# Last product of a four-layer graph network: high and low halves against a widened adjacency, with GpSimd's gathers in steps of two tiles

## The chip, the cores and the metric

The kernel runs on one core of a Trainium2 chip. The metric is the device time of one execution in microseconds (us); lower is better. The engines are TensorE (PE in the profile), VectorE (DVE), ScalarE (ACT), GpSimd (POOL) and SyncE (SP), which issues most of the DMAs. A difference of less than about 0.5% (9 us) can't be told from no change in a measurement of this kernel.

## The reference, cut to what matters

There are 4096 nodes with 128 features and a 4096 x 4096 adjacency `adj` of zeros and ones (about 0.4% ones, and the diagonal). Four layers follow one another, each added to `x`. The last is the one of the change:

```python
def _L3_gnn_ref(x, A, W1, b1, W2, b2, sigma, k):
    def _lap_mul(A, x):
        d = 1.0 / jnp.sqrt(jnp.sum(A, axis=-1))
        return d[:, None] * (A @ (d[:, None] * x))
    z = _lap_mul(A, x) @ W1 + b1
    z = jax.nn.leaky_relu(z, negative_slope=0.1)
    sq = jnp.sum(z * z, axis=-1)
    d2 = jnp.maximum(sq[:, None] + sq[None, :] - 2.0 * (z @ z.T), 0.0)
    S = jnp.exp(-jnp.sqrt(d2 + 1e-10) / (2.0 * sigma))
    ranks = ...
    S = jnp.where(ranks < k, S, 0.0)       # k = 4 nearest nodes of each row
    return _lap_mul(S + A, x) @ W2 + b2
```

The last line is a product with A, the same for all rows, and a sum of four rows for each node, weighted with S.

## The kernel before, in words

The nodes form 32 tiles (`NT`) of 128, and 8 groups (`NG`) of 4 tiles (`G`); t is a tile, g a group, q the tile in its group, r = g % 2. The adjacency is stored turned in DRAM (`adjT_panels`), one byte an entry, and comes back through the tile `panel`. Everything is written by hand: each engine has its own instruction list, and semaphores (`s_...`) join them. PE works through these stages: adjacency turned and first product (to about 330 us), the neighbourhood maximum (to 710), a wide product w = 0 (to 880), a panel product (to 1090), a wide product w = 1 (to 1228), the search of the four nearest (1228 to 1535), the last product (1518 to 1746).

**A panel product** (`product`, `blocks`, L707) takes one tile of 128 rows at a time: 32 matmuls, with a 128x128 block of the panel as weights and three bf16 parts of the features (3 x 128 = 384 columns) streaming. Bank q holds the result, VectorE adds its three parts (`take_product`, L1703). The parts come from ScalarE (`part0`, `part1`, L917 and L921) and GpSimd (`split`, L1323 and L1328). SyncE loads the panel of tile q of the next group when this group's tile q is done (512 KB).

**A wide product** (`wide_product`, L773) works on 512 rows (one group) at once: the features are the weights, in two halves (`layer_halves`, high and low), and the adjacency streams, 512 columns wide in fp32r. One *slot* is an eighth of it: a piece of 256 KB from DRAM, widened from one byte to four (`widen`, L1001 on ScalarE, L1520 on GpSimd) into a ring of 4 slots (`adj_ring`), then 8 matmuls, and `s_slot` tells that the slot is free. Slot n can be widened when slot n - 4 is free. After 8 slots ScalarE copies the product out (`take_wide`, L1008) and PE turns it back (`turn_back`, L784). Groups 0 and 1 are interleaved (`FIRST_PAIR`): pieces 0 to 5 of both, then (0,6), (1,6), (0,7), (1,7). A piece of group 1 goes to the place of the same piece of group 0, once that is widened.

**The last stage.** The scaled features are stored to DRAM (`last_operand`, L1233). GpSimd then gathers, for each tile, four times 128 rows of 512 bytes with indirect DMAs (`last_gathers`, L1573: 16 gathers a group, 128 in all) into `near`, which holds two groups. Before tile t's gathers it waits until VectorE has taken the products up to tile t - 3:

```python
pool.wait_ge(s_sum, NT + t + 2)
```

In `last_group`, at q = 2, GpSimd stages the indices of the next group (L1564), and for that waits until VectorE has used all gathered rows of the group before (`s_gath_used`); tile (g, q) also waits until (g - 2, q) is used. VectorE (`last`) takes the product of a tile, adds the four weighted rows (L2367 three times, L2370), and after four tiles scales, adds the bias and x, and ScalarE's queue stores the group (L1280).

Of the kernel before, what the change touches and what calls it, by code (L numbers as in the profile page):

```python
# [25 lines left out]
P = 128  # L26
# [17 lines left out]
ON_POOL = ((1, 2, 4, 7), (1, 4, 7))  # L44
ON_ACT = ((0, 3, 5, 6), (0, 2, 3, 5, 6))
# [7 lines left out]
def program(nc, x, adj, w0, b0, w1, w2, w31, b31, w32, b32, out):  # L53
# [5 lines left out]
    BPB = 512 // P  # L59

    ctx = ExitStack()
    with ctx:
# [15 lines left out]
        with ExitStack() as shared:  # L78
            spare = shared.enter_context(nc.sbuf_tensor("partsA", [P, NT * FW], BF16))
        ring3 = sb("adj_ring", [P, RING - 1, G, G * P], F32R)  # L80
        sb("ring_end", [P, (NT * FW * 2 - (RING - 1) * G * G * P * 4) // 4], F32)
        partsA = spare[:, :].rearrange("p (t w) -> p t w", t=NT)
        partsB = sb("partsB", [P, NT, FW], BF16)
        side = sb("side", [P, NT, F], F32)
        with ExitStack() as shared:
            rows = shared.enter_context(nc.sbuf_tensor("rows", [P, 2, N], F32))
        over_sel = rows[:, 0, 0:NT * P // 2].bitcast(BF16).rearrange("p (t s) -> p t s", t=NT)
# [279 lines left out]
        def wait_widened(eng, w, g, c):  # L367
            e, k = slot_of(g, c)
            if k in ON_POOL[w]:
                eng.wait_ge(s_wide_pool, e * len(ON_POOL[w]) + w * NG * len(ON_POOL[0]) + ON_POOL[w].index(k) + 1)  # L370
            else:
                eng.wait_ge(s_wide_act, e * len(ON_ACT[w]) + w * NG * len(ON_ACT[0]) + ON_ACT[w].index(k) + 1)

# [8 lines left out]
        def wide_slot(g, c):  # L382
            return ring[slot_of(g, c)[1] % RING].rearrange("p b (q i) -> p q b i", q=G)
# [18 lines left out]
        def _(sp):  # L402
# [105 lines left out]
            for ps in range(1, 3):  # L508
                if ps == 2:
                    for c in range(NG):  # L510
                        sp.wait_ge(s_lprod, (NG - 1) * G + c // 2 + 1)
                        load_piece(0, c)
                    other_pieces(1)

                def turn(g, peeled):
                    for q in range(G):
                        if peeled:
                            wait_widened(sp, ps - 1, NG - 1, 2 * q)
                            wait_widened(sp, ps - 1, NG - 1, 2 * q + 1)
                        else:  # L520
                            sp.wait_ge(s_lprod, (g + (ps - 1) * NG) * G + q - G + 1)
                        load_panel(g, q)
                turns(sp, turn)
# [4 lines left out]
        def _(pe):  # L528
# [238 lines left out]
            def wide_product(w, g, r, c):  # L767
# [3 lines left out]
                for b in range(G):  # L771
                    for k in range(2):
                        i = pe.matmul(bank[r][:, :], halves[:, c * G + b, k, :], ring[slot_of(g, c)[1] % RING][:, b, :],  # L773
                                      start=(c == 0 and b == 0 and k == 0), stop=(c == NG - 1 and b == G - 1 and k == 1))
                i.then_inc(s_slot, 1)

            def turn_back(w, g, r, first_pair=False):
# [5 lines left out]
                for q in range(G):  # L783
                    i = pe.transpose(bank[2 + r][:, q * P:(q + 1) * P], wideT[:, r, q * P:(q + 1) * P], ident[:, :])  # L784
# [111 lines left out]
        def _(act):  # L896
# [98 lines left out]
            def high(u, g):  # L995
                act.wait_ge(s_gsc, g + u * NG + 2)
                act.copy(halves[:, ds(g * G, G), 0, :], gsc[:, :, 0:F]).then_inc(s_p0, 1)

            def widen(w, g, c, fresh=False):
                widen_waits(act, w, g, c, "act", fresh)  # L1000
                act.copy(wide_slot(g, c), wide_source(c)).then_inc(s_wide_act, 1)  # L1001

            def take_wide(w, g, r, first_pair=False):
# [4 lines left out]
                act.copy(wideT[:, r, :], bank[r][:, :]).then_inc(s_wideT, 1)  # L1008
# [222 lines left out]
            def last_operand(g):  # L1231
# [3 lines left out]
                part0(5, g)  # L1235
# [5 lines left out]
            def turn(g, peeled, second_group=False, last=False):  # L1241
                for q in range(G):
# [11 lines left out]
                    if not peeled:  # L1254
# [4 lines left out]
                        if q == 2 and not second_group:  # L1259
                            part1(5, g - 2)  # L1260
# [15 lines left out]
            with act.Fori(0, NG // 2) as h:  # L1276
                for r in range(2):
                    g = h * 2 + r
                    act.wait_ge(s_fin, g + 1)
                    act.dma_start(out[ds(g * G * P, G * P), :].rearrange("(t p) f -> p t f", p=P),  # L1280
                                 fin[:, r, :, :]).then_inc(s_out[r], 16)
            for r in range(2):
                act.wait_ge(s_out[r], 16 * (NG // 2))
# [3 lines left out]
        def _(pool):  # L1287
# [225 lines left out]
            def low(u, g):  # L1513
                pool.wait_ge(s_p0, g + u * NG + 1)
                pool.tensor_tensor(halves[:, ds(g * G, G), 1, :], gsc[:, :, 0:F],
                                   halves[:, ds(g * G, G), 0, :].bitcast(F32), ALU.subtract).then_inc(s_rem, 1)

            def widen(w, g, c, fresh=False):
                widen_waits(pool, w, g, c, "pool", fresh)
                pool.tensor_copy(wide_slot(g, c), wide_source(c)).then_inc(s_wide_pool, 1)  # L1520
# [34 lines left out]
            with pool.Fori(0, NG) as g:  # L1555
                split(5, g)
# [42 lines left out]
        def _(dve):  # L1599
# [756 lines left out]
            def last(h, r, peeled):  # L2356
# [3 lines left out]
                dve.wait_ge(s_last, c.up())  # L2360
                for q in range(G):
                    t = g * G + q
                    take_product(5, (g + NG) * G + q, q)
                    dve.wait_ge(s_sum, (g + NG) * G + q + 5)
                    dve.wait_ge(s_gath2[r * G + q], 16 * TOP * (h + 1))
                    for k in range(TOP - 1):
                        dve.scalar_tensor_tensor(agg[:, q, 0:F], near[r * G + q][:, k, :], sg[:, q, k:k + 1],  # L2367
                                                 agg[:, q, 0:F], ALU.mult, ALU.add).then_inc(s_last, 1)
                        dve.wait_ge(s_last, c.up())
# [37 lines left out]
```

## Time and profile before

| | |
|---|---|
| median of 3 runs | 1754.88 us (1749.66 to 1757.28) |
| the profiled execution | 1755.54 us; span of its trace 1753.8 us |
| busy, share of the span | PE 88%, VectorE 72%, ScalarE 44%, GpSimd 36% |
| last product (L707, all 1024 matmuls of it) | 1518.35 to 1746.3 us |
| gathers (L1573, 128) | 1535.85 to 1739.4 us |

The times in the trace count from the start of the span. A share of busy time is a mean over stages that have different limits; for this change only the last 230 us and the wide product that came before (1092 to 1228 us) are of use.

### The profile page before, as it was taken

What the parts mean: (1) busy time and instruction counts of PE and PEld (TensorE: products, weight loads), DVE (VectorE), ACT (ScalarE), POOL (GpSimd) and SP (SyncE); (2) the same over time, 40 slices, a digit from 0 to 9 for tenths busy, and PEclk for the clock granted to TensorE, in tenths of its full rate; (3) what the DMA queues carried; (4) which work ended last, traced back from release to release, by engine and by line L of the source; (5) the groups of instructions that cost most, each with busy time, mean ns of one, the idle gap of its engine ahead of it and who ended that gap; (6) DMA issues with size and microseconds to landing.
All of it is one profiled execution on the core that took longest, in us unless ns stands there. A gap on an engine that the chain in (4) does not pass through costs nothing.

```text
span 1753.8 us, 31129 instructions
## 1 busy us (share of the span) xinstructions
PE 1538.2 (88%) x8740; PEld 920.7 (52%) x8740; DVE 1257.8 (72%) x3409; ACT 767.4 (44%) x1175; POOL 631.2 (36%) x822
## 2 busy tenths in 40 slices
PE   4999999865887888798969999999999999858997
PEld 3777777522333333576745666777444444424554
DVE  7799999964777777648856666632899999923434
ACT  3444444323555545358742223765565565500000
POOL 5333333356555556534510001333000000165664
PEclk8999999977999999899989999999999999978999
DMA  8688787523323223333303223443000000033442
GB/s 287 222 306 302 277 292 293 184 67 109 85 80 78 78 77 85 95 110 102 96 13 120 84 89 109 126 124 117 0 0 12 6 6 6 19 108 119 138 133 78
DMA packets 160459, 202.99 MB, mean 116 GB/s; under 512 B 11940, under 2 KB 133730, under 8 KB 152208
## 3 DMA queue, kind: packets, MB, share of 16 engines
q1 hardware_dynamic: 136000, 174.68, 30.0%
q0 software_dynamic: 11728, 21.33, 4.7%
q10 hardware_dynamic: 12672, 6.29, 1.2%
q8 instruction: 26, 0.43, 0.1%
q14 instruction: 33, 0.27, 0.0%
HBM read 178.85 MB, written 28.38 MB: 118 GB/s over the span
## 4 chain that ended last, share of the span: by engine, by line
PE 55%; DVE 17%; issue 16%; POOL 4%; DMA 3%; ACT 3%; DVEq 1%; POOLq 0%; ACTq 0%; SPq 0%
PE bank L707 19%; PE bank L773 9%; PE bank L585 8%; DVE partsA L2294 5%; PE bank L627 5%; PE bank L882 4%; POOL gath L1456 3%; PE bank L590 3%; PE bank L561 2%; DMA gath<-pool_features,idx_now 2%; PE bank L614 2%; DVE cand L1767 2%; PE bank L548 1%; DVE hn L1680 1%; PE bank L883 1%
## 5 line engine op out<-in xcount | busy, mean ns | idle before, releaser
L707 PE MATMUL bank<-partsB,panel 128*128 128x387 bf16 (+1 forms) x2048 | 368.2, 338 | 56.4 <-issue 34.3
L707 PEld LDWEIGHTS bank<-partsB,panel 128*128 128x128 fp8e4 x2048 | 204.5, 100 | 215.9 <-issue 74.8
L882 PE MATMUL bank<-wide,partsA 128*128 128x512 f32 x512 | 263.2, 596 | 6.3 <-ACT rows L1253 4.9
L1767 DVE MAX8 cand<-bank 128x8 f32<-128x128 f32 x1024 | 217.7, 292 | 10.4 <-PE bank L590 6.4
L984 ACT ACTIVATE first<-bank 128x512 fp8e4<-128x512 f32 x256 | 139.2, 596 | 196.1 <-PE bank L614 116.4
L627 PE MATMUL bank<-first,partsB 128*128 128x512 fp8e4 x768 | 202.7, 403 | 19.9 <-issue 17.3
L585 PE MATMUL bank<-partsA,panel 128*128 128x387 bf16 x1024 | 212.0, 329 | 6.4 <-DVE cand L1767 5.3
L1900 DVE TENSOR_TENSOR gath<-gath,bank 128x512 f32<-128x512 f32 x240 | 161.3, 683 | 76.6 <-remote 49.2
L1456 POOL DMA_INDIRECT gath<-pool_features,idx_now x160 | 171.1, 1069 | 109.3 <-DMA gath<-pool_features,idx_now 43.2
L773 PE MATMUL bank<-adj_ring,layer_halves 128*128 128x512 f32 x768 | 198.4, 409 | 8.8 <-POOL adj_ring L1520 5.4
L937 ACT ACTIVATE panel<-bank 128x1024 fp8e4<-128x1024 bf16 x128 | 131.1, 1025 | 146.4 <-PE bank L561 146.4
L1253 ACT COPY rows<-bank 128x512 f32<-128x512 f32 x256 | 133.6, 616 | 114.5 <-DVE partsA L2307 81.1
L773 PEld LDWEIGHTS bank<-adj_ring,layer_halves 128*128 128x128 f32 x768 | 146.9, 195 | 44.1 <-issue 10.9
L882 PEld LDWEIGHTS bank<-wide,partsA 128*128 128x128 f32 x512 | 95.7, 190 | 102.9 <-ACT rows L1253 55.3
L1573 POOL DMA_INDIRECT gath<-last_features,IDX x128 | 123.8, 967 | 66.2 <-issue 46.2
L627 PEld LDWEIGHTS bank<-first,partsB 128*128 128x128 bf16 x768 | 75.9, 102 | 127.1 <-issue 61.0
L1703 DVE TENSOR_REDUCE agg<-bank 128x129 f32<-128x387 f32 (+1 forms) x64 | 34.6, 558 | 149.0 <-PE bank L707 70.4
L614 PE MATMUL bank<-panel,tri 128*128 128x512 fp8e4 x256 | 82.4, 405 | 62.5 <-issue 37.7
L1323 POOL TENSOR_TENSOR rem<-gsc,partsB 128x516 f32<-128x516 f32 x23 | 26.0, 1131 | 308.5 <-ACT partsB L917 308.5
L2294 DVE MAX8 partsA<-rows 128x8 f32<-128x4096 f32 x28 | 123.6, 4415 | 6.2 <-ACT rows L1253 6.2
L1001 ACT CAST adj_ring<-panel 128x2048 fp32r<-128x2048 fp8e4 x56 | 106.0, 1904 | 45.6 <-PE bank L773 22.7
L2307 DVE FIND_INDEX8 partsA<-partsA,rows 128x8 uint32<-128x4096 f32 x28 | 123.7, 4419 | 0.0
(281 smaller groups left out, 2147.1 us busy)
## 6 DMA issues: line engine op xcount, KB each, us to landing
rows<-in_adj SPq DMA_DIRECT2D x64, 1024.0 KB, 7.2
panel<-adjT_panels SPq DMA_DIRECT2D x192, 256.0 KB
panel<-adjT_panels SPq DMA_DIRECT2D x64, 512.0 KB
adjT_panels<-panel SPq DMA_DIRECT2D x32, 512.0 KB, 3.0
gath<-pool_features,idx_now POOLq DMA_INDIRECT x160
overflow_maxima<-wide POOLq DMA_DIRECT2D x1, 2048.0 KB, 21.0
tail_maxima<-wide POOLq DMA_DIRECT2D x1, 2048.0 KB, 25.7
pool_features<-gsc ACTq DMA_DIRECT2D x8, 256.0 KB, 2.3
```

The lines of the kernel that those rows point to most:

```text
L585: i = pe.matmul(bank[q % 2][:, 0:FW], panel[:, q, j, :], parts_of[0][:, j, :], start=(j == 0), stop=(j == NT - 1))
L627: i = pe.matmul(pool_bank[(j + b) % 4][:, :], pparts[:, j + b, k * FE:k * FE + F], first_slot[:, (j + b) % SLOTS, :], start=(k == 0), stop ...
L707: i = pe.matmul(bank[q][:, 0:3 * w], panel[:, q, j, :], of_block if w < FE else parts_of[u][:, j, :], start=(j == 0), stop=(j == NT - 1))
L773: i = pe.matmul(bank[r][:, :], halves[:, c * G + b, k, :], ring[slot_of(g, c)[1] % RING][:, b, :], start=(c == 0 and b == 0 and k == 0), s ...
L882: pe.matmul(o[:, :], zs[:, q % 2, :], zT[:, c * 512:(c + 1) * 512], start=True, stop=False)
L937: act.activation(panel[:, q, c * 8:(c + 1) * 8, :].rearrange("p b i -> p (b i)"), bank[2 + c % 2][:, :].bitcast(BF16), ACT.Copy, saturate= ...
L984: i = act.activation(first_slot[:, (j + b) % SLOTS, :], tri_bank[b][:, :], ACT.Relu, saturate=False)
L1253: act.copy(rows[:, q % 2, c * 512:(c + 1) * 512], bank[c][:, :]).then_inc(s_keyrow, 1)
L1456: pool.indirect_dma_start(main[q][:, k, :], None, feat_dram, bass.IndirectOffsetOnAxis(idx_now[:, q, k:k + 1], axis=0), bounds_check=N - 1 ...
L1767: i = dve.max(cand[:, ch * BPB + b, :], bank[4 + ch % 4][:, b * P:(b + 1) * P])
L1900: i = dve.tensor_tensor(running[:, j % 2, :], running[:, j % 2, :], pool_bank[j % 4][:, :], ALU.max)
L2294: dve.max(top_v[:, q, :], rows[:, q % 2, :]).then_inc(s_top, 1)
```

## The change: what it does

1. The last product becomes a wide product, w = 2. The operands are one high and one low half (`last_high`, `last_low`) that stand where the bf16 parts and a free piece of `partsA` lay. `part1` and the three-part `split` of this stage go.
2. All 64 slots are widened by ScalarE (`ON_ACT[2]` has all 8, `ON_POOL[2]` none), into a ring of 4 slots that lies over `rows` (`last_adj_ring`), the buffer of the search of the nearest. Slots 0 and 1 wait for the search's last but one tile, slots 2 and 3 for its last.
3. VectorE's `take_product` goes: the first of the four weighted rows is added to the turned product directly from its bank, after one wait on `s_back` for the group.
4. GpSimd waits on `s_slot` instead of `s_sum`, at q = 0 and q = 2: step k of two tiles (8 gathers; k = 2g + q/2) wants 4k - 2 slots of the 64 freed. Its waits on `s_gath_used` and those for the indices stay.
5. The pieces and the output are both on SyncE's queue: the store of group g - 3 stands behind the eight pieces of group g.

```diff
-ON_POOL = ((1, 2, 4, 7), (1, 4, 7))
-ON_ACT = ((0, 3, 5, 6), (0, 2, 3, 5, 6))
+ON_POOL = ((1, 2, 4, 7), (1, 4, 7), ())
+ON_ACT = ((0, 3, 5, 6), (0, 2, 3, 5, 6), (0, 1, 2, 3, 4, 5, 6, 7))
...
+            def last_pieces(g, r):
+                for c in range(NG):
+                    wait_widened(sp, 2, g - 1, c)
+                    load_piece(g, c)
+                store_out(g - 3, r)
...
-            first_products(5, 2, None)
-            with pe.Fori(1, NG) as g:
-                for q in range(G):
-                    product(5, g, q, 2)
+            for g, c in FIRST_PAIR:
+                operand_of_pair(5, c)
+                wide_product(2, g, g, c)
+
+            def last_turn(g, r, first=False):
+                pe.wait_ge(s_wideT, g + 2 * NG - 1)
+                for c in range(NG):
+                    if first and c < 2:
+                        turn_back(2, c, c, True)
+                    if not first and c == 1:
+                        turn_back(2, g - 1, 1 - r)
+                    wide_product(2, g, r, c)
...
-            part1(5, NG - 2)
             similarities(NG - 1)
             second_std(NG - 1)
+            act.wait_ge(s_keyused, NT + 1)
+            widen(2, 0, 0)
             last_operand(NG - 1)
-            part1(5, NG - 1)
-            act.wait_ge(s_g2, 16 * NG)
...
+            widen(2, 0, 1)
+            act.wait_ge(s_keyused, NT + 2)
+            for g, c in FIRST_PAIR[2:]:
+                widen(2, g, c)
+            widen(2, 2, 0)
+            take_wide(2, 0, 0, True)
+            widen(2, 2, 1)
+            take_wide(2, 1, 1, True)
+
+            def last_turn(g, r, second=False):
+                for c in range(2 if second else 0, NG):
+                    if c == 3 and not second:
+                        take_wide(2, g - 1, 1 - r)
+                    widen(2, g, c)
...
             def last_gathers(g, r, q):
                 t = g * G + q
-                pool.wait_ge(s_sum, NT + t + 2)
+                if q % 2 == 0:
+                    pool.wait_ge(s_slot, 2 * NG * NG + g * NG + 2 * q - 2)
...
-                for q in range(G):
-                    t = g * G + q
-                    take_product(5, (g + NG) * G + q, q)
-                    dve.wait_ge(s_sum, (g + NG) * G + q + 5)
+                dve.wait_ge(s_back, g + 2 * NG + 1)
+                for q in range(G):
                     dve.wait_ge(s_gath2[r * G + q], 16 * TOP * (h + 1))
```

How the instructions stand on GpSimd at the start of the last stage (groups 0 and 1) before; `layer_product_taken` is `s_sum`, `last_features` the stored features, `gath` the gathered rows:

```order
L1564 COPY IDX<-partsA 128x16 [waits last_features_stored]
L1573 DMA gath<-last_features,IDX 128x128 [waits layer_product_taken,indices_staged]
L1573 DMA gath<-last_features,IDX 128x128 x3
L1573 DMA gath<-last_features,IDX 128x128 [waits layer_product_taken]
L1573 DMA gath<-last_features,IDX 128x128 x3
L1564 COPY IDX<-partsA 128x16
```

And the same place in the changed kernel; `ring_slot_used` is `s_slot`, `gathered_used` is `s_gath_used`:

```order
L1629 COPY IDX<-partsA 128x16 [waits last_features_stored]
L1639 DMA gath<-last_features,IDX 128x128 [waits ring_slot_used,indices_staged]
L1639 DMA gath<-last_features,IDX 128x128 x7
L1629 COPY IDX<-partsA 128x16
L1639 DMA gath<-last_features,IDX 128x128 [waits ring_slot_used]
L1639 DMA gath<-last_features,IDX 128x128 x7
L1639 DMA gath<-last_features,IDX 128x128 [waits ring_slot_used,indices_staged]
L1639 DMA gath<-last_features,IDX 128x128 x7
L1629 COPY IDX<-partsA 128x16 [waits gathered_used]
```

One wait now stands ahead of 8 gathers where before one stood ahead of 4; the waits for the use of the gathered rows are where they were.

On ScalarE the end of the search and what follows it read so before (this is group 7, the last):

```order
L1225 ACTIVATE simil<-dist 128x16 [waits distances_ready]
L1229 ACT_TABLE_LOAD
L1229 ACTIVATE second_std<-second_degree 128x4 [waits second_degree_ready]
L1233 DMA last_features<-gsc 128x4x128 [waits operand_ready]
L917 CAST partsB<-gsc 128x4x129 [waits operand_ready]
L921 CAST partsB<-rem 128x4x129 [waits remainder_ready]
L1276 UNCONDITIONAL_BRANCH [waits last_features_stored]
```

And in the changed kernel:

```order
L1285 ACTIVATE second_std<-second_degree 128x4 [waits second_degree_ready]
L1057 CAST last_adj_ring<-panel 128x4x4x128 [waits ring_slot_used,key_row_used,piece_loaded0]
L1289 DMA last_features<-gsc 128x4x128 [waits operand_ready]
L1053 CAST last_high<-gsc 128x512 [waits operand_ready]
L1057 CAST last_adj_ring<-panel 128x4x4x128 [waits piece_loaded1,ring_slot_used]
L1057 CAST last_adj_ring<-panel 128x4x4x128 [waits ring_slot_used,key_row_used,piece_loaded2]
L1057 CAST last_adj_ring<-panel 128x4x4x128 [waits piece_loaded3,ring_slot_used]
```

The first widening stands ahead of the store of the last features; after it ScalarE does nothing but widen, and copy a product out once in a group (L1064).

## Rows read from the trace of the kernel before

**Rows 1.** A window: PE, PEld, DVE, ACT, POOL busy us (instructions), clock, DMA share, GB/s.

```profile
1541.00:1568.00 27.00, 11.64 (x54) 4.94 (x51) 9.29 (x23) 0.00 (x0) 20.88 (x24) 0.72 0.42 135
```

**Rows 2.** Groups by line, 1541 to 1754 us: busy, mean ns, idle before.

```profile
L1573 POOL DMA_INDIRECT gath<-last_features,IDX x124 | 120.0, 967 | 64.5 <-issue 45.3 <-DVE agg L1703 19.2
...
L1703 DVE TENSOR_REDUCE agg<-bank 128x128 f32<-128x384 f32 x31 | 17.3, 558 | 109.2 <-remote 70.3 <-PE bank L707 30.8 <-issue 7.9
```

**Rows 3.** Timeline of the wide product w = 1: start, us, engine, line.

```profile
1149.80 3.78 ACT L1001 CAST adj_ring<-panel 128x2048 fp32r<-128x2048 fp8e4 x2 [1.62 <-issue]
...
1161.85 0.58 ACT L1008 COPY product_turned<-bank 128x512 f32<-128x512 f32 x1
...
1153.21 3.89 PE L773 MATMUL bank<-adj_ring,layer_halves 128*128 128x512 f32 x16
...
1163.44 0.60 PE L784 MATMUL bank<-ident,product_turned 128*128 128x128 f32 x4
```

**Rows 4.** Timeline, w = 1, pieces (0,6) and (1,6) of the first pair.

```profile
1109.64 2.22 POOL L1520 CAST adj_ring<-panel 128x2048 fp32r<-128x2048 fp8e4 x1 [3.66 <-PE bank L773]
...
1115.83 1.91 ACT L1001 CAST adj_ring<-panel 128x2048 fp32r<-128x2048 fp8e4 x1 [1.55 <-DMA panel<-adjT_panels]
```

**Rows 5.** Timeline where the search ends and the last product starts.

```profile
1518.35 23.00 PE L707 MATMUL bank<-partsB,panel 128*128 128x384 bf16 x128 [3.65 <-ACT rows L1253]
...
1530.19 4.42 DVE L2326 FIND_INDEX8 partsA<-partsA,rows 128x8 uint32<-128x4096 f32 x1
1530.23 0.38 ACTq L1233 DMA_DIRECT2D last_features<-gsc  x1
...
1535.85 0.99 POOL L1573 DMA_INDIRECT gath<-last_features,IDX  x1 [0.82 <-POOL IDX L1564]
```

**Rows 6.** Timeline, the longest unbroken run of gathers and PE beside it.

```profile
1543.29 6.95 PE L707 MATMUL bank<-partsB,panel 128*128 128x384 bf16 x41 [1.94 <-DMA panel<-adjT_panels]
...
1569.65 0.48 PE L707 MATMUL bank<-partsB,panel 128*128 128x384 bf16 x1 [1.62 <-issue]
...
1570.42 0.95 POOL L1573 DMA_INDIRECT gath<-last_features,IDX  x1 [0.30 <-issue]
...
1575.40 0.56 DVE L1703 TENSOR_REDUCE agg<-bank 128x128 f32<-128x384 f32 x1 [13.90 <-remote]
...
1576.77 0.95 POOL L1573 DMA_INDIRECT gath<-last_features,IDX  x1 [5.40 <-DVE agg L1703]
```

**Rows 7.** Timeline, a run of 12 gathers (first and last), VectorE's takings.

```profile
1598.42 0.97 POOL L1573 DMA_INDIRECT gath<-last_features,IDX  x1 [1.65 <-issue]
...
1612.30 0.94 POOL L1573 DMA_INDIRECT gath<-last_features,IDX  x1 [0.30 <-issue]
...
1606.95 0.56 DVE L1703 TENSOR_REDUCE agg<-bank 128x128 f32<-128x384 f32 x1 [5.10 <-remote]
1615.59 0.56 DVE L1703 TENSOR_REDUCE agg<-bank 128x128 f32<-128x384 f32 x1 [6.53 <-remote]
```

**Rows 8.** Timeline of the maximum stage: 11 indirect DMAs, PE, ScalarE.

```profile
544.28 1.00 POOL L1456 DMA_INDIRECT gath<-pool_features,idx_now  x1 [2.42 <-DMA gath<-pool_features,idx_now]
...
557.57 1.00 POOL L1456 DMA_INDIRECT gath<-pool_features,idx_now  x1 [0.30 <-issue]
...
551.39 0.59 PE L614 MATMUL bank<-panel,tri 128*128 128x512 fp8e4 x2 [0.41 <-issue]
...
558.70 1.09 ACT L984 ACTIVATE first<-bank 128x512 fp8e4<-128x512 f32 x2 [7.45 <-remote]
```

**Rows 9.** Timeline: a tile's last gather, VectorE's wait for it; the last tile.

```profile
1554.86 0.95 POOL L1573 DMA_INDIRECT gath<-last_features,IDX  x1 [0.31 <-issue]
...
1557.48 1.13 DVE L2367 SCALAR_TENSOR_TENSOR agg<-gath,sg,agg 128x128 f32<-128x128 f32 x3 [2.67 <-DMA gath<-last_features,IDX]
...
1746.91 1.13 DVE L2367 SCALAR_TENSOR_TENSOR agg<-gath,sg,agg 128x128 f32<-128x128 f32 x3
1748.07 0.35 DVE L2370 SCALAR_TENSOR_TENSOR agg<-gath,sg,agg 128x128 f32<-128x128 f32 x1
```

More of the change, by code:

```diff
@@ L79, in program @@
             spare = shared.enter_context(nc.sbuf_tensor("partsA", [P, NT * FW], BF16))
+        with ExitStack() as shared:
+            shared.enter_context(nc.sbuf_tensor("last_stage_small", [P, LAST_AT // 2], F32))
+            last_low = shared.enter_context(nc.sbuf_tensor("last_low", [P, NT, F], F32R))
         ring3 = sb("adj_ring", [P, RING - 1, G, G * P], F32R)
@@ L86, in program @@
             rows = shared.enter_context(nc.sbuf_tensor("rows", [P, 2, N], F32))
+        with ExitStack() as shared:
+            last_adj = shared.enter_context(nc.sbuf_tensor("last_adj_ring", [P, RING, G, G * P], F32R))
+        last_ring = [last_adj[:, k, :, :] for k in range(RING)]
         over_sel = rows[:, 0, 0:NT * P // 2].bitcast(BF16).rearrange("p (t s) -> p t s", t=NT)
@@ L772, in wide_product @@
                     for k in range(2):
-                        i = pe.matmul(bank[r][:, :], halves[:, c * G + b, k, :], ring[slot_of(g, c)[1] % RING][:, b, :],
+                        part = (last_high, last_low)[k][:, c * G + b, :] if w == 2 else halves[:, c * G + b, k, :]
+                        i = pe.matmul(bank[r][:, :], part, ring_of(w, g, c)[:, b, :],
                                       start=(c == 0 and b == 0 and k == 0), stop=(c == NG - 1 and b == G - 1 and k == 1))
@@ L888, in _ @@
             pe.wait_ge(s_keyrow, 8 * NT + 8)
-            first_products(5, 2, None)
-            with pe.Fori(1, NG) as g:
-                for q in range(G):
-                    product(5, g, q, 2)
+            for g, c in FIRST_PAIR:
+                operand_of_pair(5, c)
+                wide_product(2, g, g, c)
+            def last_turn(g, r, first=False):
+                pe.wait_ge(s_wideT, g + 2 * NG - 1)
+                for c in range(NG):
+                    if first and c < 2:
[3 more added lines that the diff above has]
+                    wide_product(2, g, r, c)
+            last_turn(2, 0, True)
+            last_turn(3, 1)
+            with pe.Fori(2, NG // 2) as h:
+                last_turn(2 * h, 0)
+                last_turn(2 * h + 1, 1)
+            turn_back(2, NG - 1, 1)
         @block.scalar
@@ L1268, in _ @@
             last_operand(NG - 2)
-            part1(5, NG - 2)
             similarities(NG - 1)
             second_std(NG - 1)
+            act.wait_ge(s_keyused, NT + 1)
+            widen(2, 0, 0)
             last_operand(NG - 1)
-            part1(5, NG - 1)
-            act.wait_ge(s_g2, 16 * NG)
[L1276 to L1283, printed above, removed]
+            widen(2, 0, 1)
[11 more added lines that the diff above has]
+                    widen(2, g, c)
+            last_turn(2, 0, True)
+            last_turn(3, 1)
+            with act.Fori(2, NG // 2) as h:
+                last_turn(2 * h, 0)
+                last_turn(2 * h + 1, 1)
+            take_wide(2, NG - 1, 1)
         @block.gpsimd
@@ L1555, in _ @@
             with pool.Fori(0, NG) as g:
-                split(5, g)
+                low(5, g)
             pool.wait_ge(s_g2, 16 * NG)
```

86 lines of the change are left out of this document (56 added, 30 removed).

## The prediction

> **What bounds the kernel now.** I read the windows over the last stage first. From 1541 to 1568 us PE was busy 11.64 us of 27 at a mean clock of 0.72, while GpSimd was busy 20.88 us [rows 1]: PE, the engine with the most busy time in the kernel, isn't what sets the pace there. The groups by line say who waits: VectorE's taking of a product waited 109.2 us, 70.3 of it for "remote", a signal whose sender the profile doesn't name, and GpSimd waited 64.5 us between its gathers [rows 2]. Then I read the timeline around the longest of these waits.
>
> A panel product needs 6.95/41 = 0.17 us a matmul, so the first tile of group 1, begun at 1543.29, is done at 1548.7. VectorE, idle for 13.90 us, got it at 1575.40. In between PE issued a matmul every one or two microseconds without waiting for a semaphore. GpSimd had issued 28 gathers without a pause from 1535.85 on, and the last ended at 1571.37: the signal came 4.0 us after that [rows 5, 6]. The same in small: a run of 12 gathers from 1598.42 to 1613.24; a product signalled 8.5 us into it came through, the next one came at 1615.59, 2.4 us after the run's end [rows 7]. And in an earlier stage, with other matmuls: PE's pair ended at 551.98, 7.7 us into a run of 11 indirect DMAs, and ScalarE got it at 558.70, 0.1 us after the run's end at 558.57 [rows 8]. So while GpSimd gathers without a pause for more than about 8.5 us, PE's signals stand until the run ends, and PE soon stands too. I call this the hold. It bounds the last stage now: gathers have a period of (1612.30 - 1598.42)/11 = 1.26 us [rows 7], 20.2 us for the 16 of a group, PE needs 128 x 0.17 = 21.7 us, but the last 88 gathers took 141 us (1598.42 to 1739.4), which is 25.6 us a group.
>
> **What the change removes.** The PE work of a group falls from 21.7 to 16.2 us: 8 slots of 3.89/2 = 1.95 us and one turning back of 0.60 [rows 3]. VectorE loses 0.56 us a tile, of no worth, since it waits anyway. The removed `part1` and third parts lie behind VectorE's search; without them GpSimd may start its gathers a little sooner, while their store now stands behind one widening of 1.9 us: I take 1535 in place of 1535.85 [rows 5].
>
> **What it adds.** ScalarE, idle in this stage before, needs 8 x 1.89 + 0.58 = 15.7 us a group [rows 3], about as much as PE. Both are under GpSimd's 20.2 + 0.2 for staging the indices = 20.4. So GpSimd bounds the stage in any case, and the most that the change can give is its gathers without waits: 128 x 1.26 + 1.6 = 163 us.
>
> PE's start moves back: before it began at 1518.35 [rows 5], now it waits for the ring's place, the search's buffer, free at 1530.19 + 4.42 = 1534.6 for slots 2 and 3. From there 14 widenings (26.5 us) end the first pair, with two loads that nothing covers: pieces (1,6) and (1,7) can be loaded only when (0,6) and (0,7) are widened, and that took from 1111.86 to 1115.83, 4.0 us [rows 4]. One widening more, the copy and the turning back make 1534.6 + 26.5 + 8.0 + 3.1 = 1572.2. VectorE's four tiles take 4 x 1.5 = 6.0 us [rows 9]. That matters, because GpSimd wants all of group 0 used before step 3 (group 1, q = 2), which it reaches at 1535 + 3 x 10.15 = 1565.5. Without any hold it waits there until 1578.2, 12.7 us. Behind it stand 104 of the 128 gathers.
>
> The new waits on freed slots cost nothing by themselves: step k wants 4k - 2 slots, and PE frees 5 in the 10.15 us of a step. The store on SyncE's queue stands ahead of the next group's pieces, but the group that it stores (g - 3) has been gathered by then; nothing.
>
> A piece comes in rows of 512 bytes, a panel in rows of 4 KB, both 2 MB a group. In the wide product w = 1 the same pieces kept PE going, 16 matmuls in 3.89 us [rows 3], and after the first pair a piece is asked for a group (16 us) ahead, four times its 4.0 us [rows 4]: so nothing. The Trainium skill (DMA: Bandwidth & Descriptors, "Why small descriptors are slow (HBM only)") says that small descriptors cost bandwidth by fixed cycles a packet; were a piece twice as slow beside gathers, the two uncovered loads would add 8 us, and the rest would still be hidden.
>
> **The hold in the new order.** A step of two tiles is 10.15 us, longer than 8.5, and nothing makes GpSimd pause between steps when the slots are there. What hangs on PE's signals is more than before: ScalarE widens only 4 slots beyond the last freed slot that it knows, and copies a product out only when it knows that it is complete; PE stops one slot into the next group until that copy is there. Followed through:
> - Steps 0 and 1 run from 1535 to 1555.3. Signals stand from 1543.5 on, with 5 slots known; step 2 wants 6 and waits for the signals to about 1557.5. PE stops at slot 9 at about 1552. Seven slots (13.7 us), the two loads (8.0) and copy and turning (1.2) end at 1580.4, VectorE's tiles at 1586. Step 3 starts there, not at 1578.
> - Steps 3 to 6 pass in one run, to 1627, since their slots are known. Step 7 wants group 2 used, whose turning back was signalled within the run: 2.4 us for the signals, 6.0 for VectorE, some 0.6 of its own lag, 1636.
> - From there a pair of steps costs 20.4 us and, when the group's last slot fell behind the 8.5 us, also 2.4 (signal) + 1.2 (copy, turning) + 6.0 (VectorE) = 9.6: 30.0. The bounds are 20.4 and 30.0; the nearest row is the pace of before, 25.6. I take 26.5, because a step now is longer than 8.5 us and the chain behind a signal is longer. Four pairs: 1742 for the start of step 15.
> - Step 15 ends at 1752. Then the signals (2.4), copy and turning of group 7 (1.2), VectorE's tiles (6.0), and the 5.4 us that now lie between the last weighted row, 1748.42 [rows 9], and the end of the span at 1753.8: 1767. The profiled execution is 1.7 us longer than its span: 1769 us, against 1755.54 for the one profiled before, whose median of three, 1754.88, is practically the same.
>
> **The rivals.**
> - *No hold (0.18).* For it: PE gives 16 instructions in 1.95 us, 8.2 a us, in place of 2 in 0.17, 11.8 a us [rows 3, 6], and ScalarE paces it. Against it: the maximum stage, where PE had gaps [rows 8]. Time: 1535 + 163 + 12.7 = 1711 for the last gather's end, 1.7 us until it is used (1555.81 to 1557.48), 1.5 for the tile, 5.4, 1.7: 1721 us. This is the other side: it decides if PE's signals come through in a run of more than 20 us.
> - *The hold comes later (0.22).* If it grows with PE's own instructions, it starts 8.5 x 11.8/8.2 = 12.2 us into a run. Then a group's last slot is signalled in time in nearly each pair, and only the first pair and one long run pay: 1586 + 13 x 10.15 = 1718, one wait of 9.6, 1.7 + 1.5 + 5.4 + 1.7: 1738 us. The Trainium skill (NOTIFIC — the notification-queue block, "7.1 Overflow: three behaviours, one of which stalls the engine") says that the block's internal pipeline pushes back on its producer instead of losing a record, which can throttle an engine; by it a slower stream of PE instructions is held later, and the time is this rival's. The trace speaks against it: the maximum stage, whose PE had gaps, was held no later than the panel product [rows 7, 8].
> - *PE stays slow as well (0.08).* After its stop PE's clock was low (mean 0.72, which mixes the two levels 1.2 and 2.4 GHz) [rows 1]. If each pair's 16.2 us of PE work runs half of it at 1.2 GHz, 8 us more, pairs cost over 30: 1636 + 4 x 34 + 10 + 15 + 1.7 = 1799 us.
> - *The waits nearly balance (0.07).* Pairs of 23 us: 1755 us, no change.
>
> **How the numbers follow.** The hold as in my sum has 0.45: 1769 us, from 1757 (pairs of 23.5) to 1783 (of 30.0). Faster by over 0.5% (below 1746) is no hold and most of the later hold: 0.38. Within 0.5%, about what a measurement of this kernel can tell from no change: the balance, a part of the later hold, and the low end of the likeliest: 0.17. Slower (above 1763.7): 0.45. The range that leaves out no more than 2 in 10 reaches from no hold to above the full price: 1719 to 1786.
>
> **What would show it.** In the new profile: GpSimd's gathers in runs of 16 or more with pauses of 8 to 10 us between them, at the odd steps; ScalarE's widening or PE's slots standing from about 8.5 us into a run to 2 us after it; VectorE waiting for the turning back and not for gathers; the first pause of GpSimd ending near 1586. I am wrong if PE's slots follow at 2 us within runs of 20 us (then 1721 to 1738), if the first pair ends near 1572, or if the stage's gathers take 1.3 us each after step 3. If gathers no longer set the end and PE does, the reading of the stage is wrong altogether.

## The result, and the profile after

The changed kernel took 1766.55 us (median of 10, 1758.50 to 1782.67), the kernel before 1752.68 us beside it (median of 10): ratio 1.0102, 95% interval 1.0076 to 1.0127. It is about 1% slower, by 14 us.

The windows of the changed kernel (columns as in [rows 1]), one in the first pair of groups and one in the third group:

```profile
1541.00:1568.00 27.00, 13.36 (x52) 10.21 (x50) 0.00 (x0) 10.63 (x6) 17.98 (x20) 0.80 0.42 112
1616.00:1643.00 27.00, 5.30 (x11) 3.27 (x12) 7.69 (x20) 5.01 (x3) 16.92 (x19) 0.50 0.20 52
```

Between 1616 and 1643 us PE, ScalarE and VectorE together are busy for 18 us of 27 while GpSimd gathers; PE's granted clock is at its lower level (0.50, 1.2 GHz) after its stop. The groups by line from 1535 to 1765 us say who waits:

```profile
L1639 POOL DMA_INDIRECT gath<-last_features,IDX x128 | 122.9, 960 | 51.5 <-issue 46.2 <-remote 5.0 <-PE bank L814 0.3
L1057 ACT CAST last_adj_ring<-panel 128x2048 fp32r<-128x2048 fp8e4 x62 | 113.8, 1898 | 93.1 <-remote 59.5 <-issue 16.4 <-PE bank L814 9.9
L2431 DVE SCALAR_TENSOR_TENSOR agg<-gath,sg,bank 128x128 f32<-128x128 f32 x32 | 11.0, 344 | 154.0 <-remote 54.9 <-PE bank L825 52.2 <-issue 39.4
```

The 109.2 us that VectorE waited for products, 70.3 of them "remote" [rows 2], have become 93.1 us of ScalarE before its widenings (59.5 remote) and 154.0 us of VectorE for the turning back, of which 52.2 are its one wait for the first product. The timelines show how they lie. GpSimd's gathers, first and last of the first two runs and of the end:

```profile
1534.48 0.99 POOL L1639 DMA_INDIRECT gath<-last_features,IDX  x1 [0.82 <-issue]
1563.39 0.94 POOL L1639 DMA_INDIRECT gath<-last_features,IDX  x1 [0.30 <-issue]
1594.53 1.35 POOL L1639 DMA_INDIRECT gath<-last_features,IDX  x1 [0.16 <-issue]
1634.11 0.95 POOL L1639 DMA_INDIRECT gath<-last_features,IDX  x1 [0.30 <-issue]
1640.60 0.96 POOL L1639 DMA_INDIRECT gath<-last_features,IDX  x1 [4.99 <-remote]
...
1743.33 1.18 POOL L1639 DMA_INDIRECT gath<-last_features,IDX  x1 [3.52 <-issue]
1752.31 0.94 POOL L1639 DMA_INDIRECT gath<-last_features,IDX  x1 [0.30 <-issue]
```

and ScalarE's widenings where it had waited:

```profile
1552.30 1.90 ACT L1057 CAST last_adj_ring<-panel 128x2048 fp32r<-128x2048 fp8e4 x1 [4.26 <-issue]
1566.30 1.90 ACT L1057 CAST last_adj_ring<-panel 128x2048 fp32r<-128x2048 fp8e4 x1 [12.11 <-remote]
...
1575.14 3.71 ACT L1057 CAST last_adj_ring<-panel 128x2048 fp32r<-128x2048 fp8e4 x2 [2.98 <-DMA panel<-adjT_panels]
1581.68 3.70 ACT L1057 CAST last_adj_ring<-panel 128x2048 fp32r<-128x2048 fp8e4 x2 [2.83 <-DMA panel<-adjT_panels]
1618.80 1.90 ACT L1057 CAST last_adj_ring<-panel 128x2048 fp32r<-128x2048 fp8e4 x1 [12.17 <-issue]
1639.89 10.90 ACT L1057 CAST last_adj_ring<-panel 128x2048 fp32r<-128x2048 fp8e4 x6 [19.20 <-remote]
```

The first run of 24 gathers ends at 1564.3 and ScalarE goes on at 1566.30; the second, of 32, ends at 1635.1 and ScalarE goes on at 1639.89. Between 1606.6 and 1639.9 it widened a single slot. VectorE's first weighted row of the first, the third and the last group:

```profile
1587.69 0.35 DVE L2431 SCALAR_TENSOR_TENSOR agg<-gath,sg,bank 128x128 f32<-128x128 f32 x1 [52.21 <-PE bank L825]
...
1627.93 0.35 DVE L2431 SCALAR_TENSOR_TENSOR agg<-gath,sg,bank 128x128 f32<-128x128 f32 x1 [16.27 <-remote]
...
1753.69 0.35 DVE L2431 SCALAR_TENSOR_TENSOR agg<-gath,sg,bank 128x128 f32<-128x128 f32 x1 [8.64 <-issue]
```

The first is released by the turning back, as predicted; the last starts 0.4 us after GpSimd is done with issuing the last gather (1752.31 + 0.94).

### The profile page after: what moved, and what is told of

Read it like the earlier page. It is cut to its first block, busy times and chain, and to the rows that moved or that the text cites. A ratio compares the mean times of both kernels' runs of the same rounds, so it can differ in the third digit from the quotient of the medians.

```text
span 1764.8 us, 30270 instructions
## 1 busy us (share of the span) xinstructions
PE 1485.4 (84%) x8260; PEld 926.8 (53%) x8260; DVE 1236.7 (70%) x3377; ACT 882.7 (50%) x1239; POOL 619.7 (35%) x814
## 4 chain that ended last, share of the span: by engine, by line
PE 49%; DVE 19%; issue 16%; another core or an unknown queue 7%; ACT 4%; POOL 2%; DVEq 1%; DMA 1%; ACTq 0%; POOLq 0%; SPq 0%
PE bank L814 9%; PE bank L747 8%; PE bank L625 8%; PE bank L667 8%; DVE partsA L2360 5%; PE bank L923 4%; PE bank L654 3%; PE bank L630 3%; PE bank L601 2%; POOL gath L1639 2%; DVE cand L1833 1%; PE bank L588 1%; ACT first L1039 1%; DVE partsA L2387 1%
## 5 line engine op out<-in xcount | busy, mean ns | idle before, releaser
L1966 DVE TENSOR_TENSOR gath<-gath,bank 128x512 f32<-128x512 f32 x240 | 160.5, 679 | 94.6 <-remote 38.6
L667 PE MATMUL bank<-first,partsB 128*128 128x512 fp8e4 x768 | 200.1, 399 | 22.5 <-issue 20.6
L747 PE MATMUL bank<-partsB,panel 128*128 128x387 bf16 x1024 | 176.5, 332 | 16.5 <-POOL partsB L1392 15.6
L814 PE MATMUL bank<-last_adj_ring,last_high 128*128 128x512 f32 x256 | 111.8, 437 | 83.3 <-ACT last_adj_ring L1057 55.3
L1057 ACT CAST last_adj_ring<-panel 128x2048 fp32r<-128x2048 fp8e4 x64 | 117.6, 1898 | 93.1 <-remote 59.5
L747 PEld LDWEIGHTS bank<-partsB,panel 128*128 128x128 fp8e4 x1024 | 101.0, 99 | 87.5 <-issue 11.1
```

Of the source, the lines that this page charges most:

```text
L667: i = pe.matmul(pool_bank[(j + b) % 4][:, :], pparts[:, j + b, k * FE:k * FE + F], first_slot[:, (j + b) % SLOTS, :], start=(k == 0), stop ...
L747: i = pe.matmul(bank[q][:, 0:3 * w], panel[:, q, j, :], of_block if w < FE else parts_of[u][:, j, :], start=(j == 0), stop=(j == NT - 1))
L814: i = pe.matmul(bank[r][:, :], part, ring_of(w, g, c)[:, b, :], start=(c == 0 and b == 0 and k == 0), stop=(c == NG - 1 and b == G - 1 and ...
L1057: act.copy(wide_slot(w, g, c), wide_source(c)).then_inc(s_wide_act, 1)
L1966: i = dve.tensor_tensor(running[:, j % 2, :], running[:, j % 2, :], pool_bank[j % 4][:, :], ALU.max)
```

## The experiments

### The held signal and the chips

The runs fell on several chips, and these turned out to be of two kinds. So each time stands beside that of the kernel before on the same chip, which took either about 1700 us ("open chip" below) or about 1755 us ("holding chip"). One chip was used twice, half an hour apart, and was open both times; two others were holding, and so was the one of the first comparison, by its times and its traces. The first four kernels ran on an open chip.

**One gather of four.** GpSimd issues one gather a tile; VectorE weights that row four times. The other three gathered rows are left out.

```diff
-                for k in range(TOP):
+                for k in range(1):
                     pool.indirect_dma_start(near[r * G + q][:, k, :], ...
```

> Leaves out three of the four gathered rows of every tile: GpSimd issues one indirect gather a tile, two a step (2.5 us), and VectorE weights that one row four times. So no run of gathers is long. My theory (an unbroken run of gathers holds TensorE's signals): no hold here; the first pair of groups ends at about 1572, the others at TensorE's 16.2 us a group, so 1572 + 6 x 16.2 + 1.2 + 6.0 + 5.4 + 1.7 = 1684 us. Rival (TensorE and ScalarE are slow in this stage by themselves, by the clock, by the pieces' loads or by VectorE's shared ports): groups of 22 us or more as in the changed kernel, 1720 to 1740 us.

1666.84 us beside 1700.35 (ratio 0.981, 0.9781 to 0.9838). ScalarE's copies of the finished products (start, us):

```profile
1575.23 0.59 ACT L1064 COPY last_turned<-bank 128x512 f32<-128x512 f32 x1
1590.11 0.59 ACT L1064 COPY last_turned<-bank 128x512 f32<-128x512 f32 x1
1605.00 0.60 ACT L1064 COPY last_turned<-bank 128x512 f32<-128x512 f32 x1
1620.00 0.57 ACT L1064 COPY last_turned<-bank 128x512 f32<-128x512 f32 x1
```

A group takes 15.0 us, less than the 16.2 that I had put for PE, and the whole kernel is 17 us under my 1684. What PE and ScalarE can do was not the limit. As this chip is an open one, the run doesn't test the hold.

**Wait for the landing, behind each step and behind each tile.**

```diff
+                if q % 2 == 1:        # second kernel: behind every tile
+                    pool.wait_ge(s_gath2[r * G + q], 16 * TOP * (e + 1))
```

> The changed kernel, and GpSimd waits after each step of two tiles (8 gathers, 10.2 us) until that step has landed: 16 pauses of about 2.2 us. Nothing else is changed and all work is done. My theory: TensorE's signals come through in each pause, so a step takes 10.15 + 2.2 = 12.4 us, 16 of them 198 us, and step 3 waits some 7 us for the first group: last gather at 1534.5 + 198 + 7 = 1740, end 1740 + 1.5 + 1.5 + 5.4 + 1.7 = 1750 us, faster than the changed kernel (1766.5). Rival (TensorE's standing does not come from the unbroken run): the pauses come on top of the waits, 1766 + 16 x 2.2 less what falls together, 1780 to 1800 us.

> As the run before, but the wait for the landing stands behind each tile (4 gathers, 5.1 us). My theory: no run is over 5.1 us, so nothing is ever held, TensorE works through at 16 to 17 us a group, and GpSimd alone bounds: 32 x (5.1 + 2.2) = 234 us, end 1534.5 + 234 + 3 + 5.4 + 1.7 = 1778 us, with TensorE's last product done long before. Rival: TensorE still stands for stretches of 10 us and the time is over 1800 us.

1747.94 us (ratio 1.0279, 1.025 to 1.0308) and 1783.32 us (1.0491, 1.0462 to 1.052), beside the same 1700.35. The times are near my numbers, but they say only what the pauses cost GpSimd on a chip that holds nothing.

**A copy between the tiles.** GpSimd copies 128x1024 f32 behind each tile's four gathers; all the kernel's work is done.

```diff
                                             ).then_inc(s_gath2[r * G + q], 16)
+                if not (isinstance(g, int) and g + q == 0):
+                    pool.wait_ge(s_fill, t)
+                pool.sem_inc(waited["pool"], 1)
+                pool.tensor_copy(gath[:, 1, 16:24, :], last_low[:, 0:8, :].bitcast(F32)).then_inc(s_fill, 1)
```

> The changed kernel, and GpSimd copies 128x1024 f32 from on-chip memory to on-chip memory (estimate 1 to 2 us, from its 1.13 us for 128x516) behind each tile, waiting for nothing but its own copy before. It parts two forms of my theory. If it is enough that no gather is issued for a microsecond or two, the signals come through every 6 to 7 us, and the stage is GpSimd's alone: 163 + 32 x 1.5 = 211 us plus a few us of waits, end 1755 to 1765 us with TensorE never standing longer than some us. If GpSimd must stand idle (or its gathers must land), the runs grow by the copies and the hold with them: 1790 us or more.

1736.60 us (ratio 1.0211, 1.0179 to 1.0242), under both of my ranges. That the kernel before took 52 us less than at first had to be explained, and the maximum stage did it. Its code is the same in every kernel here. The groups by line of this run:

```profile
L1971 DVE TENSOR_TENSOR gath<-gath,bank 128x512 f32<-128x512 f32 x240 | 160.7, 680 | 15.1 <-PE bank L668 13.8
```

The same group waited 76.6 us in the profile of before and waited 94.6 us in that of after, 49.2 and 38.6 of them remote. No engine waits for an unnamed signal anywhere in that stage here.

**Both kernels again.** They fell on a holding chip.

> The changed kernel as it is. In the last four runs the kernel before took 1700 us where it took 1753 beside the changed kernel, and the maximum stage (the same code in all of them) showed no waits for an unnamed signal. So the hold may be a thing of the chip or of the moment. If it is absent here: first gather at 1524.5, steps 0 to 2 to 1554, step 3 after the first group is used at about 1569, 104 gathers of 1.26 us to 1700, and 8.6 us behind them: 1709 us, against 1700 for the kernel before (ratio 1.005). If the hold is there for this kernel though not for the one before (my theory as first written, with the run's length deciding): 1750 us or more.

> The kernel before as it is, for its trace under the same conditions. If the hold is absent: no waits for an unnamed signal in the maximum stage or in the last one, the gathers of the last stage in one run at 1.26 us each from about 1526 to 1689, time 1700 us. If its 1700 us come from something else (a clock, an earlier stage), the last stage still shows the pauses of 10 us or more between the gathers, at 25.6 us a group.

1768.27 us for the changed kernel (ratio 1.0070, 1.0044 to 1.0096) and 1754.19 for the one before (0.9992, 0.9969 to 1.0014, against its other runs). VectorE's takings in the kernel before, 1535 to 1752 us:

```profile
L1703 DVE TENSOR_REDUCE agg<-bank 128x128 f32<-128x384 f32 x32 | 17.8, 557 | 112.7 <-remote 95.1 <-PE bank L707 17.2
```

So the hold is there in both kernels on this chip, and the 1700 us of the kernel before on an open chip are its time without the hold. GpSimd's timeline of the changed kernel, where it had waited:

```profile
1557.67 0.95 POOL L1639 DMA_INDIRECT gath<-last_features,IDX  x1 [3.76 <-remote]
...
1586.93 1.35 POOL L1639 DMA_INDIRECT gath<-last_features,IDX  x1 [0.16 <-issue]
1633.30 0.96 POOL L1639 DMA_INDIRECT gath<-last_features,IDX  x1 [1.65 <-remote]
```

### What breaks the hold

The copy between the tiles was run once more, this time on a holding chip together with the changed kernel.

> The changed kernel as it is, once more, since the runs so far fell on two kinds of chip: on one, beside a kernel before of 1700 us, no engine ever waited for an unnamed signal; on the other, beside one of 1755 us, TensorE's signals were held. If the kernel before takes about 1700 us here, no hold: 1709 us for this one, ratio 1.005, its only loss the wait before step 3 (about 15 us) less some us at the end. If the kernel before takes 1755 us: 1768 us again, ratio 1.007 to 1.010.

> The changed kernel with a copy of 128x1024 f32 on GpSimd behind each tile of four gathers, once more (it measured 1737 us beside a kernel before of 1700 us, 1.021). If the kernel before takes 1755 us here, the hold is present, and the two forms of my theory part: if a break of 1.2 us in the issue of gathers is enough to let the signals through, it measures as where there is no hold, 9 us later for the longer maximum stage, 1745 to 1750 us and faster than the changed kernel, with ScalarE never waiting over 5 us; if GpSimd must be idle, or waiting, for the signals to pass, the runs are now of 12 us a step and longer in all, and the time is 1790 us or more. If the kernel before takes 1700 us here: 1737 us again.

The changed kernel took 1776.09 us (ratio 1.0117, 1.0092 to 1.0142), with the copies 1746.82 us (0.9943, 0.9919 to 0.9968): 29 us less, though GpSimd has 33.5 us more to do. Groups by line of the changed kernel, 1535 us to the end:

```profile
L1639 POOL DMA_INDIRECT gath<-last_features,IDX x127 | 122.1, 962 | 49.4 <-issue 42.5 <-remote 6.9
L1057 ACT CAST last_adj_ring<-panel 128x2048 fp32r<-128x2048 fp8e4 x62 | 114.0, 1900 | 105.8 <-remote 75.8 <-PE bank L814 13.0 <-issue 9.5
```

and with the copies:

```profile
L1058 ACT CAST last_adj_ring<-panel 128x2048 fp32r<-128x2048 fp8e4 x63 | 115.4, 1901 | 24.9 <-PE bank L815 16.1 <-issue 3.5 <-DMA panel<-adjT_panels 3.0
L1646 POOL COPY gath<-last_low 128x1024 f32<-128x1024 f32 x32 | 33.5, 1046 | 0.1
...
L1971 DVE TENSOR_TENSOR gath<-gath,bank 128x512 f32<-128x512 f32 x240 | 160.5, 679 | 103.4 <-remote 61.1 <-PE bank L668 37.0 <-issue 3.3
```

(The last row is the maximum stage, from the whole span.) In one and the same execution VectorE waits 61.1 us for unnamed signals in the maximum stage, whose gathers have no copy between them, and the last stage isn't held: ScalarE's wait falls from 105.8 to 24.9 us, and with the same copies on the open chip it was 24.0. Its longest single wait was 8.8 us, for PE, where I had expected none over 5; on the open chip it was 9.1. The break is small. GpSimd's timeline:

```profile
1540.52 0.95 POOL L1640 DMA_INDIRECT gath<-last_features,IDX  x1 [0.30 <-issue]
1541.47 1.05 POOL L1646 COPY gath<-last_low 128x1024 f32<-128x1024 f32 x1
1542.69 0.97 POOL L1640 DMA_INDIRECT gath<-last_features,IDX  x1 [0.17 <-POOL gath L1646]
```

But for 6.5 us before step 3, where it waits for VectorE, GpSimd hardly stands idle; it only issues no gather for 1.2 us every 6 us. The edit also puts a wait for GpSimd's own last copy before each copy; the copy and this wait were not tried apart. The first gather comes 9.7 us later than on the open chip (1536.72 against 1526.99) and the whole kernel is 10.2 us longer: by these numbers nothing of the hold is left in the last stage.

### Without the gate, and with a third set of buffers

Both ran on the holding chip of the two kernels above, where the changed kernel took 1768.27 us. First, without GpSimd's wait for freed slots:

```diff
-                if q % 2 == 0:
-                    pool.wait_ge(s_slot, 2 * NG * NG + g * NG + 2 * q - 2)
```

> The changed kernel without GpSimd's wait for TensorE's freed ring slots. My sum put these waits at nothing by themselves: the same time as the changed kernel, within 3 us, with or without the hold. The rival (the steps pace GpSimd) makes this kernel 10 us or more faster.

1792.15 us (ratio 1.0218, 1.0186 to 1.0249), 24 us slower than with the gate. ScalarE's waits:

```profile
1619.21 1.90 ACT L1057 CAST last_adj_ring<-panel 128x2048 fp32r<-128x2048 fp8e4 x1 [10.26 <-issue]
1652.17 1.90 ACT L1057 CAST last_adj_ring<-panel 128x2048 fp32r<-128x2048 fp8e4 x1 [31.06 <-remote]
...
1664.80 1.90 ACT L1057 CAST last_adj_ring<-panel 128x2048 fp32r<-128x2048 fp8e4 x1 [10.74 <-remote]
```

They lie in and behind a run of 48 gathers, from 1596.86 to 1657.57. Both of my expectations missed: the gate isn't free of effect, and taking it away doesn't make the kernel faster either. With it the longest run is 32 gathers.

Second, three sets of buffers for gathered rows and for indices, so that step 3 doesn't wait for the first group (the loops over groups on GpSimd and VectorE are written out, and four counters that nobody waits for share one semaphore):

```diff
-        near = [gath[:, i // G, ...] for i in range(2 * G)]
+        near = ([gath[:, i // G, ...] for i in range(2 * G)]
+                + [gath[:, i // 2, (G + i % 2) * TOP:(G + i % 2 + 1) * TOP, :] for i in range(G)])
...
-                        if not (first_pair and r == 0):
-                            pool.wait_ge(s_gath_used, NT + g * G + 4)
-                        stage_near(g + 1, 1 - r)
+                        if g >= 2:
+                            pool.wait_ge(s_gath_used, NT + (g - 1) * G + 4)
+                        stage_near(g + 1, (g + 1) % 3)
```

> The changed kernel with three sets of buffers for the gathered rows and three of indices in place of two, so that step 3 no longer waits until the first group is used (and the loops over groups of this stage are written out on GpSimd and VectorE). Without the hold: step 3 follows step 2 at once, and nothing waits behind it, since group 3 wants group 0 used only 12 steps in: the stage is 128 gathers, 1524.5 + 163 + 8.6 = 1697 us, 12 us less than the changed kernel. If the wait before step 3 costs nothing (because the end is set by something else): the same as the changed kernel. With the hold: longer runs, no gain, 1760 us or more.

1746.54 us (ratio 0.9946, 0.9925 to 0.9966): 22 us faster than the changed kernel, where I expected nothing on a holding chip. GpSimd's gathers that had waited:

```profile
1559.37 0.94 POOL L1640 DMA_INDIRECT gath<-last_features,IDX  x1 [3.81 <-remote]
...
1582.90 0.94 POOL L1640 DMA_INDIRECT gath<-last_features,IDX  x1 [3.79 <-remote]
...
1606.77 0.94 POOL L1640 DMA_INDIRECT gath<-last_features,IDX  x1 [3.14 <-issue]
```

No run here is longer than 16 gathers. My expectation had the longer runs from the missing wait. I read it the other way round now: it is the 30 us wait before step 3 that lets PE run ahead, and so opens the gate for the 32 gathers behind it. Without that wait there is a pause after every 16 gathers (once after 8), six times of 2.4 to 3.8 us and twice of 8.9, and signals pass in them; ScalarE waits 56.0 us in place of 90.5. The longest run and the time go together: 16 gathers 1747 us, 32 gathers 1768, 48 gathers 1792. That the length is the cause isn't shown by this: they are three kernels, and the third set of buffers also takes away the wait before step 3 itself, which I had put at 12 us where nothing is held. How much of the 22 us is that and how much the shorter runs stays open, as this kernel didn't run on an open chip.

### What the change is worth with the breaks

Third set of buffers and a copy of half the size behind each tile; and the kernel before with that same copy. They fell on an open chip.

```diff
+                pool.tensor_copy(rem[:, :, 0:F], ...).then_inc(s_fill, 1)
```

> The changed kernel with the third set of buffers (no wait before step 3) and a copy of 128x512 f32 on GpSimd behind each tile, half of the copy that undid the hold before: some 0.5 us of work, a break of about 0.6 us. A copy of 0.2 us between two gathers, the staging of the indices, doesn't end the hold, one of 1.05 us does, so this size is open. If it does: gathers 160 + 32 x 0.6 = 180 us from 1536, 1716 for the last one's end, 11.5 us from there to the end of the span as in the changed kernel, and 1.7: 1730 us, ratio 0.985, and no wait for an unnamed signal in the last stage. If it is too short a break: as the kernel with third buffers alone plus the copies, 1755 us or more. If the kernel before takes 1700 us on this chip (no hold): 1719 us, ratio 1.011.

> The kernel before, its panel product and its order untouched, with the same copy of 128x512 f32 behind each tile of four gathers. It asks what the change is worth where nothing is held. If the break ends the hold, this kernel too is bound by GpSimd alone: 1535 + 180 = 1715 us for the last gather's end, 11.5 to 14 us behind it, 1.7: 1728 to 1731 us, ratio 0.985, the same as the kernel beside it, and the new product and the steps gain nothing of their own. If the change's faster product counts once the hold is gone, this kernel is 5 us or more slower than the other. If the break is too short: 1770 us, slower than before by the copies.

1715.55 us (ratio 1.0086, 1.0061 to 1.0110) and 1714.83 us (1.0088, 1.0061 to 1.0115), beside 1700.57. The groups by line of the second, the kernel before with copies, from 1525 us:

```profile
L1574 POOL DMA_INDIRECT gath<-last_features,IDX x128 | 124.3, 971 | 35.2 <-issue 29.7 <-POOL rem L1580 4.0 <-POOL IDX L1565 0.8
L1580 POOL COPY rem<-gath 128x512 f32<-128x512 f32 x32 | 20.6, 643 | 0.1
L1708 DVE TENSOR_REDUCE agg<-bank 128x128 f32<-128x384 f32 x32 | 17.7, 552 | 5.5 <-PE bank L708 4.6
```

The wait for the products is 5.5 us here; on a holding chip, without copies, it was 112.7. With either product the stage is 128 gathers and 32 copies of GpSimd, and the two kernels take the same time: with the copies, and where nothing is held, the wide product gains nothing. Without the copies this wasn't measured. PE's panel product ended at 1689.3 us in the second kernel; an estimate for its gathers without the copies is 1705.6 - 20.6 = 1685 us, so there PE and GpSimd would end nearly together. Whether a copy of 0.64 us breaks the hold was not seen, as nothing was held there. Nor did the kernel before run with copies on a holding chip, so what the wide product is worth there once the hold is broken stays open too. So no version measured here was found faster than the kernel before on both kinds of chip: on holding ones the copies (0.9943) and the third set (0.9946) are, by little more than 0.5%; on an open one no kernel that does all the work was.

## Why the prediction was right, point by point

- **The hold bounds the stage.** Right, by a run that removes it. My wording was too absolute in two ways. It belongs to the chip, not to the kernel. And it isn't closed until the run's end: a signal or two pass within a long run (ScalarE at 1618.80, 24 us into a run, and without the gate at 1652.17, 55 us into one), and after that run of 48 gathers ScalarE waited another 7.2 us.
- **"Steps 0-1 run to 1555.3, step 2 waits to 1557.5, step 3 starts at 1586."** In the profile after, step 2 didn't wait: the signal it wanted came (ScalarE goes on at 1552.30), the run went on to 1564.3, the release came at 1566.30 in place of 1557.5, and step 3 started at 1594.53, 8.5 us late. In the second profile of the same kernel step 2 started at 1557.67 and step 3 at 1586.93, as in my sum. In a third one step 2 waited 1.7 us, and step 3 started at 1594.27 all the same. Which signals pass differs from execution to execution, and this fits the changed kernel's wide spread, 24 us over 10 runs.
- **The first pair.** The two loads that nothing covers cost 2.98 and 2.83 us, not 4.0 each. In the run with one gather of four, 33.1 us lie between ScalarE's first widening behind the search (1523.18) and the copy of the first product (1556.27), where my terms make 26.5 + 8.0 + 1.9 = 36.4.
- **"Step 7 at 1636."** Started at 1640.60. The start of the run was late by 8.5 us, but the wait behind it was 5.5 us and not 9.0, since VectorE got group 2 at 1627.93, within the run.
- **"26.5 us per pair of steps."** (1743.33 - 1640.60)/4 = 25.7. With step 15 at 1743.3 for 1742 and the gathers' end at 1753.3 for 1752, two errors of some us took each other out: that is luck. The pauses weren't those that I named, 8 to 10 us at the odd steps: behind step 3 they were 5.5, 9.9, 4.8, 4.8 and 3.5 us, before steps 7, 9, 12, 13 and 15, and two of the runs had only 8 gathers.
- **The end.** 15.0 us from the last gather to the end of the span were predicted, 11.5 measured here. In the two repetitions it was 23 and 25 us: there the last product itself was late (VectorE waited 26.13 us for the last turning back, until 1758.70). So the medians of the repetitions, 1768 and 1776 us, are near the predicted 1769 with another division, and my sum had no term for that case.
- **The waits on freed slots "cost nothing by themselves".** Wrong: with them the kernel is 24 us faster on a holding chip. That they do it by ending runs is my reading of the traces.
- **The rivals.** "No hold", 1721 us, is what an open chip has, with what I hadn't seen: the kernel before is then 1700 us and not 1755. The changed kernel wasn't timed there. That its result fell on a holding chip, like the trace from which I predicted, was luck. An estimate from its run with copies: 26 of them lie behind step 3, 1.2 us each, 1736.6 - 31 = 1705 us, no change within 0.5%; that is argued, not shown. "The hold comes later" would have left one wait behind step 3; there were five. Profiled executions are held little more than others, if at all: on holding chips they lie within 4 us of the medians (1752.8 us for the kernel before against 1754.2, 1779.8 for the third run of the changed one against 1776.1), and the profiles of the open chip show no hold. The Trainium skill (NOTIFIC — the notification-queue block, "7.1 Overflow: three behaviours, one of which stalls the engine") says that the block's internal pipeline pushes back rather than lose a record, which can throttle an engine; these numbers give that no support as the cause. "PE stays slow" was only a small part of the price. After its stops PE was at 1.2 GHz (0.50 from 1616 to 1643), but over the whole stage a matmul of the high half took 434 ns and one of the low half 424, against 413 and 409 with the copies on a holding chip: 256 x 0.036 = 9 us in all, where the rival had 8 us in each of four pairs.

## What to carry to other kernels

A wait whose sender the profile doesn't name, ending a microsecond or two behind a long series of GpSimd's gathers, may be removed by breaking the series, even with useless work of 1 us; so put GpSimd's other work between gathers and not before or behind them. Before a faster product is built, remove the hold and see what bounds the stage then: here, with copies between them, the gathers decided, whichever product stood beside them. And run the kernel before again beside every experiment, and read a stage that no edit touches: its waits told the chips apart.

## What the runs showed of the hardware

- Chips differ: the same kernel before took 1700 us on one and 1753 to 1756 us on the others (medians), and VectorE's waits for unnamed signals in the maximum stage were 0 in all profiles of the one and 32 to 61 us in those of the others. Why they differ stays open, and so does by what way gathers hold back the signals.
- A copy of 0.20 us between two gathers (the staging of indices, at 16 gathers' distance) doesn't end the hold; one of 1.05 us every four gathers, with its wait, does. Where between them the point lies wasn't measured on a holding chip.
- Part of the waiting in long runs is put down to nothing that the profile shows (16.4 us of ScalarE and 39.4 of VectorE, "issue" in the groups of after). Whether signals of other engines than PE are held too isn't shown.
